# One order of steps per engine in the mixing stage of a four-batch transformer layer, with the second chunk's up products, the late score units and the first batch's set-up moved

## What is computed

```
x = x + layernorm(attention(layernorm(x)))
x = x + layernorm(ffn(layernorm(x)))
attention: q, k, v = split(x @ w_qkv.T + b_qkv); rope(q), rope(k)
           out = softmax(mask(q @ k.T / 4)) @ v;  out @ w_out.T + b_out
ffn:       hidden = fwht(silu(x @ W1.T) * (x @ W3.T));  hidden @ W2.T
```

## Time and profile before

| | us |
|---|---|
| median of 3 runs | 500.68 |
| lowest and highest | 498.67, 501.37 |
| the profiled execution, whole | 497.78 |
| its span, first to last instruction | 496.1 |
| until the first head of the first batch | 80.3 |
| mixing stage of the second batch | 28.8 |
| a whole batch in the middle | 106.7 |

### The profile page before, as it was taken

The page is one execution under the profiler, slowest core; times in us unless marked ns, Lnnn a source line. Parts: engine busy times, 40 slices in busy tenths (PEclk is TensorE's granted clock), DMA queues, the critical chain, the costliest instruction groups (busy, mean ns, idle before and its releaser), DMA issues.

```text
span 496.1 us, 7892 instructions
## 1 busy us (share of the span) xinstructions
PE 405.0 (82%) x2884; PEld 338.2 (68%) x2884; DVE 281.2 (57%) x936; ACT 210.9 (43%) x314; POOL 162.1 (33%) x284
## 2 busy tenths in 40 slices
PE   1679677999599997988599988987799979858992
PEld 1569645558489985557499975566699965448991
DVE  7554583625937776536856776267576754273114
ACT  4445234753323337843423347813332367423221
POOL 4136002533512226514422235614132245321232
PEclk9999865999969999999889999999799999997998
DMA  6549900000397000200695001102880002000001
GB/s 230 215 136 247 212 1 1 2 2 0 127 255 171 1 1 1 85 1 1 179 245 130 1 1 42 44 1 72 219 201 21 1 1 85 1 1 1 1 1 42
DMA packets 35463, 36.95 MB, mean 74 GB/s; under 512 B 2016, under 2 KB 34528, under 8 KB 35424
## 3 DMA queue, kind: packets, MB, share of 16 engines
q1 hardware_dynamic: 35424, 36.45, 26.6%
HBM read 21.76 MB, written 14.68 MB: 73 GB/s over the span
## 4 chain that ended last, share of the span: by engine, by line
PE 58%; DVE 13%; DMA 9%; issue 7%; ACT 6%; SPq 3%; POOL 2%; DVEq 0%; POOLq 0%; ACTq 0%
PE ps L266 30%; PE ps L448 8%; PE ps L464 7%; PE ps L436 5%; DMA qk_scratch<-qk_s 4%; DMA q_t<-qk_scratch 4%; ACT probs L656 4%; DVE masked_scores L923 2%; SPq L293 2%; DMA raw_bias<-in_b_out 2%; PE ps L498 2%; DVE xy L985 1%; POOL hid_s L803 1%; PE ps L405 1%; DVE stats_h L870 1%
## 5 line engine op out<-in xcount | busy, mean ns | idle before, releaser
L923 DVE CUSTOM_DVE_ANT_0 masked_scores<-ps,mask_row 128x128 bf16<-128x128 f32 (+3 forms) x256 | 114.4, 488 | 61.6 <-PE ps L436 61.1
L266 PE MATMUL ps<-xt,w_s 128*128 128x256 f32 x768 | 111.7, 294 | 0.0
L266 PEld LDWEIGHTS ps<-xt,w_s 128*128 128x128 f32 x768 | 106.2, 202 | 0.5
L803 POOL TENSOR_TENSOR hid_s<-gate,hid_s 128x512 fp32r<-128x512 f32 x32 | 41.2, 1287 | 135.9 <-ACT hid_s L668 135.9
L656 ACT ACTIVATE probs<-ps 128x1280 f32<-128x1280 f32 x64 | 76.4, 1242 | 9.5 <-PE ps L448 8.9
L436 PE MATMUL ps<-k_t,q_t 96*128 96x128 f32 (+3 forms) x256 | 71.7, 356 | 9.8 <-DMA q_t<-qk_scratch 5.6
L448 PEld LDWEIGHTS ps<-q_t,k_t 128*128 128x128 f32 x256 | 44.9, 198 | 32.2 <-ACT probs L656 14.7
L266 PE MATMUL ps<-w_s,hid_s 128*128 128x256 f32 x384 | 55.5, 284 | 7.0 <-POOL hid_s L803 7.0
L448 PE MATMUL ps<-q_t,k_t 128*128 128x512 f32 (+3 forms) x256 | 55.7, 345 | 5.6 <-ACT probs L656 4.0
L266 PEld LDWEIGHTS ps<-w_s,hid_s 128*128 128x128 f32 x384 | 51.6, 190 | 9.3 <-POOL hid_s L803 8.7
L436 PEld LDWEIGHTS ps<-k_t,q_t 96*128 96x128 f32 x256 | 43.0, 198 | 18.6 <-DVE maxima L923 10.9
(11 more groups left out here) (99 smaller groups left out, 485.3 us busy)
## 6 DMA issues: line engine op xcount, KB each, us to landing
qk_scratch<-qk_s SPq DMA_DIRECT2D x32, 256.0 KB, 5.6
k_t<-qk_scratch SPq DMA_DIRECT2D x16, 384.0 KB, 5.5
q_t<-qk_scratch SPq DMA_DIRECT2D x8, 768.0 KB, 8.8
qk_scratch<-qk_s SPq DMA_DIRECT2D x8, 512.0 KB, 5.5
xa<-in_x SPq DMA_DIRECT2D x4, 512.0 KB, 9.6
xy<-in_x SPq DMA_DIRECT2D x4, 512.0 KB, 3.5
out<-xy SPq DMA_DIRECT2D x8, 256.0 KB, 2.3
o_t<-in_w SPq DMA_DIRECT2D x1, 1024.0 KB, 10.0
```

The costliest lines, as they stand in the source:

```text
L266: ins = eng.matmul(o, lhs(i), rhs(j), start=first and n == 0, stop=last and n == 2, skip_group_check=skip)
L803: pool.tensor_tensor(hid_s[:, a % 2, 1, :], gate[:, a % 2, :], hid_s[:, a % 2, 0, :].bitcast(F32), ALU.subtract).then_inc(S["hid_l"], 1)
L923: ins = dve.tensor_tensor_reduce(masked_scores[:, SCORE_NO[n] % 2, i * keys:(i + 1) * keys], ps[:, banks[n], i * keys:(i + 1) * keys], mas ...
```

## The change

1. `MIX`, `MIX_LAST` and `FIRST_MIX` become tables with one order for each engine. The value product is parted from the one for queries and keys (step `b`, `values_product`), and `rot_s` gets a second buffer. PSUM banks of `H` change.
2. `u4` and `u5`, the first two quarters of the second hidden chunk's up products (`AHEAD`), are made in the mixing stage; `feed_forward` leaves them out.
3. `UNITS_AFTER` is another table; the units ahead are still 41, and the 14th comes later.
4. The tail's score units stand one behind a head from head 2 on, where they stood in pairs from head 4; the first value product waits for all maxima but one.
5. The start: x is loaded first, 14 products of zeros stand ahead of TensorE's first turn, the split of the weights is dealt out anew, queries and keys go ahead of values, and SP waits for the first half's fetch before it stores the second half (first batch alone).
6. The transform of W2: its outer three steps are now additions and subtractions of whole rows on POOL (`butterflies`), and TensorE does 16 products in place of 128, behind score unit 33. ACT and DVE split the result later; DVE's splits of W3 and W1 (2048 columns each) and of the transformed W2 move into the first attention stage.

```diff
-H_BANK = [5, 3, 5, 3]
+H_BANK = [6, 5, 4, 5]
...
-TAIL_AFTER = {4: (0, 2), 5: (2, 4), 6: (4, 6), 7: (6, 7)}
+TAIL_AFTER = {2: (0, 1), 3: (1, 2), 4: (2, 4), 5: (4, 5), 6: (5, 6), 7: (6, 7)}
...
-MIX = """o0 o1 d0 d1 n0 n1 q0 l0 l1 e0 c0 o2 d2 y0 o3 s0 n2 y1 l2 d3 s1 n3 y2 v0 l3 q1 r0 y3 s2 s3 e1 c1 t0
...
+MIX = {
+    "PE": """o0 q0 o1 n0 o2 n1 y0 b0 o3 n2 b1 y1 n3 q1 y2 r0 y3 q2 b2 r1 q3 b3 r2 r3 H0 H1 u0 u1 u4 H2
+        H3 u2 u3 u5""".split(),
+    "ACT": """n0 q0 n1 b0 n2 n3 q1 b1 r0 S q2 r1 q3 b2 r2 r3 H0 H1 b3 H2 H3 u3""".split(),
+    "DVE": """o0 d0 o1 d1 l0 c0 o2 d2 o3 l1 s0 d3 r0 s1 l2 l3 v0 s2 c1 R0 s3 r1 R1 v1 t0 w0 c2 R2 t1 R3
+        w1 r2 N0 N1 N2 c3 N3 r3 t2 t3 L0 L1 L2 L3""".split(),
...
+    "PE": """o0 o1 n0 n1 o2 y0 n2 o3 y1 n3 y2 y3 H0 H1 u0 u1 u4 u5 H2 H3 u2 u3""".split(),
...
-UNITS_AFTER = [(0, 0, 0), (3, 2, 0), (2, 3, 0), (4, 1, 0), (4, 2, 0), (4, 3, 0), (4, 3, 0), (4, 1, 0), (0, 0, 1)]
+UNITS_AFTER = [(0, 0, 0), (4, 2, 0), (4, 0, 0), (2, 0, 0), (6, 2, 0), (7, 2, 0), (4, 1, 0), (4, 3, 0), (0, 0, 0)]
+AHEAD = [(1, 0), (1, 1)]
-FIRST_SELECTOR = [None, 0, 2, 9]
-FIRST_TRANSFORM = [-1, -1, -1, -1, -1, 4, 8, 13]
-FIRST_W2_PARTS = [14, 19]
+FIRST_SELECTOR = {2: 0, 3: 2}
+BUTTERFLIES_BEFORE = [0, 4, 13]
+FIRST_W2_PARTS = {"split": 18, "transform": 33, "words": 36, "high": 38}
...
+                    if b == 0:
+                        sp.wait_ge(S["qk_in"], 48)
...
+            load_x(0)
-            load_x(0)
-            sp.wait_ge(S["split_l"], 4)
+            sp.wait_ge(S["w3_l"], 1)
...
+                pe.wait_ge(S["xt_l"], b * TILES + t + 1)
+                if t >= 2:
+                    pe.wait_ge(S["qk_copied"], b * TILES + t - 1)
...
+            def values_product(b, t):
...
-                        pe.wait_ge(S["maxed"], (b + 1) * N_SCORES)
+                        pe.wait_ge(S["maxed"], (b + 1) * N_SCORES - 1)
...
-                    if kind == "up":
+                    if kind == "up" and (n, i) not in AHEAD:
-            def transform(c):
-                for i in range(HCH):
-                    sign = bin(i & c).count("1") % 2
-                    for s in range(2):
-                        ins = pe.matmul(ps[:, c // 2, (c % 2) * DIM:(c % 2) * DIM + DIM], had_s[:, sign, :],
-                                        w2_s[:, s, i, :], start=(c % 2 == 0 and i == 0 and s == 0),
-                                        stop=(c % 2 == 1 and i == HCH - 1 and s == 1), skip_group_check=True)
+            def transform():
+                pe.wait_ge(S["had_made"], 1)
+                pe.wait_ge(S["w2_l"], 2)
+                for c in range(HCH):
+                    for part in range(2):
+                        ins = pe.matmul(ps[:, c // 2, (c % 2) * DIM:(c % 2) * DIM + DIM], had_s[:, :],
+                                        w2_s[:, part, c, :], start=(c % 2 == 0 and part == 0),
+                                        stop=(c % 2 == 1 and part == 1), skip_group_check=True)
+            pe.wait_ge(S["zeroed"], 2)
+            for n in range(14):
+                pe.matmul(bank(7), k_t[0:QK_ROWS, 0, 0:P], k_t[0:QK_ROWS, 1, :], start=True, stop=True, skip_group_check=True)
+            pe.wait_ge(S["wqkv_l"], 2)
+            mix(-1, FIRST_MIX["PE"])
-                for c in range(HCH):
-                    if FIRST_TRANSFORM[c] == n:
-                        transform(c)
+                if n == FIRST_W2_PARTS["transform"]:
+                    pe.wait_ge(S["v_copied"], TILES)
+                    transform()
-            pe.wait_ge(S["split_l"], 4)
-            pe.wait_ge(S["transformed_l"], 1)
+            pe.wait_ge(S["transformed_words"], 1)
-                mix(b, MIX)
+                if b == 0:
+                    pe.wait_ge(S["wo_l"], 1)
+                    pe.wait_ge(S["out_bias"], 2)
+                    pe.wait_ge(S["w1_l"], 1)
+                    pe.wait_ge(S["w3_l"], 1)
+                    pe.wait_ge(S["transformed_l"], 1)
+                mix(b, MIX["PE"])
...
+            select(1)
+            act.wait_ge(S["bias_in"], 32)
+            act.activation(bias_h[:, 0:3 * DIM], raw_bias[:, 0:3 * DIM], ACT.Copy).then_inc(S["bias_h"], 1)
+            act.activation(bias_s[0:P // 2, 0:3 * DIM], raw_bias[0:P // 2, 0:3 * DIM], ACT.Copy).then_inc(S["bias_s"], 1)
+            mix(-1, FIRST_MIX["ACT"])
...
+                if n == FIRST_W2_PARTS["split"]:
+                    act.wait_ge(S["w2_turned"], 3)
+                    act.activation(w2_s[:, 0, :, :].rearrange("p c n -> p (c n)"), mixed_w2, ACT.Copy).then_inc(S["w2_h"], 1)
+                if n == FIRST_W2_PARTS["words"]:
+                    act.wait_ge(S["transformed"], 1)
+                    act.activation(raw_w2, ps[:, 0:4, :].rearrange("p a n -> p (a n)"), ACT.Copy, scale=W2_SCALE)\
+                       .then_inc(S["transformed_words"], 1)
+                if n == FIRST_W2_PARTS["high"]:
+                    act.wait_ge(S["transformed_words"], 1)
+                    act.activation(w2_s[:, 0, :, :].rearrange("p c n -> p (c n)"), raw_w2, ACT.Copy)\
...
-                if t >= 1:
-                    pool.wait_ge(S["rotated"], b * TILES + t)
-                o = rot_s.rearrange("p (h e i) -> p h e i", e=2, i=HALF)
+                if t >= 2:
+                    pool.wait_ge(S["rotated"], b * TILES + t - 1)
+                o = (rot_s, rot_s_odd)[t % 2].rearrange("p (h e i) -> p h e i", e=2, i=HALF)
...
+            def butterflies(n):
+                src, dst = (raw_w2, mixed_w2) if n % 2 == 0 else (mixed_w2, raw_w2)
+                if n == 0:
+                    pool.wait_ge(S["w2_in"], 16)
+                    pool.wait_ge(S["wqkv_l"], 2)
+                    pool.wait_ge(S["wo_l"], 1)
+                else:
+                    pool.wait_ge(S["w2_turned"], n)
+                a, o = (w.rearrange("p (u e n) -> p u e n", e=2, n=DIM << n) for w in (src, dst))
+                pool.tensor_tensor(o[:, :, 0, :], a[:, :, 0, :], a[:, :, 1, :], ALU.add)
+                pool.tensor_tensor(o[:, :, 1, :], a[:, :, 0, :], a[:, :, 1, :], ALU.subtract).then_inc(S["w2_turned"], 1)
+            def w2_low(half):
+                rows = slice(half * HCH // 2, (half + 1) * HCH // 2)
+                words = slice(half * HCH * DIM // 2, (half + 1) * HCH * DIM // 2)
+                pool.wait_ge(S["w2_h"], 1)
+                pool.tensor_tensor(w2_s[:, 1, rows, :].rearrange("p c n -> p (c n)"), mixed_w2[:, words],
+                                   w2_s[:, 0, rows, :].rearrange("p c n -> p (c n)").bitcast(F32), ALU.subtract)\
+                    .then_inc(S["w2_l"], 1)
+            pool.memset(sixty_fourth[:, :].bitcast(F32), 2.0 / P).then_inc(S["sixty_made"], 1)
+            pool.wait_ge(S["split_h"], 1)
+            pool.tensor_tensor(wqkv_s[:, 1, 1, :], raw_wqkv[:, 3 * DIM:6 * DIM], wqkv_s[:, 0, 1, :].bitcast(F32), ALU.subtract)\
+                .then_inc(S["wqkv_l"], 1)
+            for m in FIRST_MIX["POOL"]:
+                if n in BUTTERFLIES_BEFORE:
+                    butterflies(BUTTERFLIES_BEFORE.index(n))
+                if n in (FIRST_W2_PARTS["split"], FIRST_W2_PARTS["split"] + 2):
+                    w2_low((n - FIRST_W2_PARTS["split"]) // 2)
...
+                if order is MIX:
+                    layer_x(b + 1)
+                    split(w2_s, raw_w2, "transformed_h", 1, "transformed_l")
+                    split(w3_s, raw_w3, "split_h", 4, "w3_l")
+                    dve.wait_ge(S["transformed_l"], 1)
+                if b == 0:
+                    split(w1_s, raw_w1, "split_h", 3, "w1_l")
+                mix(b, order["DVE"])
```

172 lines of the change are left out of this document (86 added, 86 removed).

## The result

The changed kernel takes 497.21 us (median of 8 runs, 495.60 to 497.88) against 499.69 us before (8 runs, 498.67 to 501.37): ratio 0.9945, 95% interval 0.9926 to 0.9963. The prediction was 487.7 us with a range of 479 to 496. The sign was right, the size was not: 2.5 us came of 13.0.

What follows compares the result with a forecast made beforehand. Room was seen in the mixing stages, the set-up and single waits. Set-up -4.8, tail -5.5, mixing -3.9, feed-forward -1.7 and last batch +2.9 sum to -13.0 us: 487.7 us as a median, range 479 to 496.

Steps and rivals of the forecast that it cites:

- Set-up, -4.8: Start to first head: earlier second half and two removed waits, less costs of the new transform and ACT passes; -4.8 us.
- the added wait on SP costs 2.0 of the 5.3: Set-up: first store leaves 5.3 us earlier, but transfers in line take 31.7 in place of 29.7 us.
- POOL's butterflies: Set-up: three passes plus W2's low part at 2.25 ns a column beside DVE's maxima, 18.5 us of POOL.
- The rival of a slow POOL: Set-up: butterflies at 5.8 ns a column beside DVE, block behind unit 33 waits, 17 us more, 504.5; chance 0.06.
- Splits at no cost in the first attention stage: First attention stage: DVE's three added passes of 2.3 us cost nothing; 1 to 2 us if the cover failed.
- the tail's own term: Attention stages: single tail units start the first value product earlier, 1.5 us in three batches, 1.0 in the first; -5.5.
- Mixing stages, -3.9: Three mixing stages: first score unit 2.4 us earlier, less about 1.1 taken back, 1.3 each; -3.9, between 0 and -10.
- the layout by hand that gave 244.7 as first quarter: Mixing stage: both engines' new orders laid side by side from 218.5; first up product at 244.7 in place of 247.2.
- that takes back about 1.1: Mixing stage end: first 18 products in the thin stretch and a gap behind them take back about 1.1 us.
- Feed-forward, -1.7: Feed-forward stages: 0.24 us in each of three from one more unit ahead of `down`, and a 1.01 us fetch wait gone.
- Last batch, +2.9: Last batch's mixing stage: only half of 48 products stand before the last two turns, so `down` starts later; +2.9 us.
- The rival Less: Whole kernel: new waits replace old; mixing stages bring nothing, tail half, set-up 3; 496.1 us, chance 0.15.

Runs made afterwards that it cites:

- The four corrections: Changed kernel with norm tiles 2 and 3 turned before the quarters, rotation before norms, no SyncE fetch wait, W1/W3 splits in DVE's set-up: 480.60 us, ratio 0.9649.
- the run with POOL's short products: Changed kernel, but POOL makes only 1 of 16 heads of tile 3's products in the mixing stages (result not the reference's): 498.04 us, ratio 0.9965.
- the run with the rotation first: Changed kernel with norm tiles 2 and 3 turned before the quarters, plus tile 3's rotation before two norms and POOL's products before the last root: 485.81 us, ratio 0.9732.
- the turns first: Changed kernel, but TensorE turns norm tiles 2 and 3 ahead of the first quarter, six quarters in a row, last batch too: 490.53 us, ratio 0.9834.

## Why the prediction was wrong, step by step

**What bounds the kernel.** Right: the room was in the mixing stages, the set-up and single waits. The four corrections took 16.6 us out of just these by the medians, 14.8 by the ratios.

**Set-up, -4.8, measured -1.4.** First product at 13.73 and first copy at 16.21 in place of 13.0 and 15.4, then rotations of 1.2 us beside POOL's products where I had 0.7: the first store left at 25.88, not 24.2. The failed step is "the added wait on SP costs 2.0 of the 5.3". In it the second store had the 6.0 us of the first; alone it took 7.76, and 6.7 to 7.5 in the other kernels with the wait. The two fetches took 9.8 each, as forecast, so the four parts in line took 33.2 us (25.88 to 59.11) and not 31.7, and without the wait 29.5: it cost 3.7 in this pair, some 3 over all traces. The 13.9 us of the earlier trace rows, which I called the fetch with the store beside it, is the time between two issues, with the second store's end in it; the fetch loses nothing beside the store (41.69 against 41.66), the store does. That misreading left the total of 29.7 right but hid that a wait could gain nothing. Behind the landing I had 18.8 us and it took 19.85: DVE idled 3.22 us beside the transform, not 2.4.

**POOL's butterflies.** Right: 2.34 us per 1024 columns beside maxima. The rival of a slow POOL did not happen, and the block behind unit 33 waited 0.39 us for POOL. That an instruction of DVE with a single input from SBUF doesn't meet POOL held for the maxima; it doesn't hold for all such instructions: the norm, with one tensor from SBUF, took 0.79 us beside POOL's products and 0.41 without.

**Splits at no cost in the first attention stage.** Wrong by the 1 to 2 us that I had named as the price if the cover failed: 1.6 us. The cover was DVE's own idle time; the cost arose on POOL, whose low part of maxima took 2.02 us beside the split, and TensorE waited for it. That is most of why the attention stages showed 4.0 in place of 5.5. Alone the tail gave 5.2 in the stages and 6.3 in the medians, so the tail's own term and its mechanism were right: the first value product of the third batch stands 8.19 us behind its first head (294.01 to 302.20), inside the 8 to 8.6 that I had named.

**Mixing stages, -3.9, measured +3.2.** Two steps failed. The first is the layout by hand that gave 244.7 as first quarter, 26.2 us behind the first `o`; it was 28.0. In it operations had their undisturbed length (0.9 us per stage too little, by the run with POOL's short products), and the low part of rotated tile 2 stood behind others with TensorE waiting for it (some 0.6 us, by difference to the run with the rotation first). The other 0.3 stay open. DVE was to idle for about 5 us; it idled for 7.5 of the 28.0, past the 7 that I had named as a sign of being wrong. The second is "that takes back about 1.1" for the clock. First quarter to first unit grew by 1.7 to 2.1 us where 1.2 were forecast: the first 18 products ran at the low clock nearly throughout (3.79 to 4.2 us), and the gap behind them came on top.
**Feed-forward, -1.7, measured -2.8.** Two of the three stages became 0.5 us shorter, where I had 0.24. The third became 1.9 shorter; it had held before's fetch wait of 1.01. With the old units but the new tail that stage took 42.93 us without any such wait, so that wait came and went with the execution, and I don't count its going as shown. No run took the new table of units alone.

**Last batch, +2.9, measured +4.1.** Mechanism and place right, wait for `hid_l` 1.98 us as named (2). Of the 4.1, the two groups of 24 products took 1.1 us more than the 48 before (5.26 and 3.14 against 7.28), the gap between them is 1.5, and the wait for `hid_l` grew by 1.4. The forecast had 3.9 us for the first 24 products and no term for the low clock there; that is the missing 1.2. With the turns first 3.1 of the 4.1 go.

**The rival Less** had the time, 496.1, but not the reasons: it took the mixing stages at nothing and halved the tail. I had given it 0.15 and ended the range at its figure; the measured 497.2 lies beyond because the mixing stages, the set-up and the last batch came out worse than it had them (+3.2, -1.4 and +4.1 against 0, -3 and +2.9), though the attention stages came out better (-4.0 against -2.7). That the time fell so near to its figure is chance. A mixing stage can become longer, and I had allowed 0 as its worst end.

## What to carry to other kernels

When an order is laid out by hand from measured durations, ask of each operation what runs beside it on the shared port, and of each result that another engine waits for why it isn't first. Don't read the time between two issues as the duration of one transfer, and don't give a transfer in a new place the duration it had in another. Before an early finish is counted, look at what the engine meets there: here a long wait for a fetch, with the low clock behind it, turned being early into a loss. And before a stage's gain or loss is put down to an edit, look at the same stage in other runs that share its code: here one differed by 2.3 us.

## What I had not expected of the hardware

- A store of five transfers beside a fetch left the fetch's landing unchanged (41.69 against 41.66 us), though both go through HBM. The store paid: 11.1 us to its end beside the fetch, 7.8 alone.
- DVE and POOL slow each other in both directions: DVE's cosine product 1.20 in place of 0.69 us beside POOL's products, DVE's norm 0.79 in place of 0.41 beside the same, POOL's low part of six maxima 2.02 in place of 0.28 beside DVE's split, POOL's root of two numbers 1.21 in place of 0.69 beside DVE's rotation and norm.
- 22 products of 256 columns in a thin stretch kept the granted clock at 1.00 and made the 48 products behind it take 5.99 us; in the same kernel without them 48 took 7.6 to 8.3. A wait of 3.53 us was followed by 6.1 us at 0.50; behind waits of 1.56 and 1.15 us in the same execution it stayed at 1.00.
